# Sparse attention in a four-layer kernel: masked sums before head sums on VectorE, and a new order of the sums and gathers on GpSimd

## The reference, cut to what matters

```
iq = (x @ w_iq.T + b_iq).reshape(B, S, 4, 64);  ik = x @ w_ik.T + b_ik
iw = x @ w_iw.T + b_iw                                  # 4 weights for each query
head_scores  = relu(einsum('bqhd,bkd->bhqk', iq, ik))   # 4 heads, S x S each
index_scores = einsum('bhqk,bqh->bqk', head_scores, iw) # weighted sum of the heads
top_idx = top_k(index_scores, 32)
logits = einsum('bqd,bkd->bqk', rope(Q), rope(K)) * scale   # -inf where not in top_idx
x = x + softmax(logits) @ V @ w_o.T + b_o
```

## Time and profile before

| | us |
|---|---|
| median of 3 runs | 523.01 (522.72 to 523.64) |
| the profiled execution | 523.16 |
| its span, first to last instruction | 521.3 |

### The profile page before, as it was taken

The page is one execution under the profiler, slowest core; times in us unless marked ns, Lnnn a source line. Parts: engine busy times, 40 slices in busy tenths (PEclk is TensorE's granted clock), DMA queues, the critical chain, the costliest instruction groups (busy, mean ns, idle before and its releaser), DMA issues. The chain is left out here.

```text
span 521.3 us, 11629 instructions
## 1 busy us (share of the span) xinstructions
PE 437.5 (84%) x3048; PEld 383.1 (73%) x3048; DVE 377.2 (72%) x1501; ACT 337.8 (65%) x934; POOL 290.4 (56%) x329
## 2 busy tenths in 40 slices
PE   2689995799999896999988999998876599999981
PEld 1579894788988885667767777776655599988981
DVE  4789984836666651389999999999997656666661
ACT  1458882146766641899998999999782117666750
POOL 4763442067540005698878888887660027677752
PEclk9989996789999998999999999999996579999997
DMA  8942222124431111001111111111001213222210
GB/s 228 289 163 79 65 82 82 1 73 110 110 90 43 34 37 32 4 17 32 31 31 32 32 45 48 31 32 31 21 21 42 22 27 107 78 77 79 67 42 20
DMA packets 45070, 32.42 MB, mean 62 GB/s; under 512 B 13524, under 2 KB 39508, under 8 KB 45012
## 3 DMA queue, kind: packets, MB, share of 16 engines
q1 hardware_dynamic: 39892, 19.11, 13.1%
q0 software_dynamic: 5120, 12.62, 9.2%
HBM read 19.10 MB, written 12.62 MB: 61 GB/s over the span
## 5 line engine op out<-in xcount | busy, mean ns | idle before, releaser
L427 POOL DMA_INDIRECT big<-rows,gidx x64 | 61.6, 963 | 56.7 <-DVE gidx L1152 28.3
L639 PE MATMUL bank<-WE,hT 128*128 x624 | 83.6, 277 | 7.5 <-ACT hT L849 6.0
L629 PE MATMUL bank<-X,w 128*128 x624 | 83.4, 277 | 1.2 <-ACT X L836 0.4
L639 PEld LDWEIGHTS bank<-WE,hT 128*128 128x128 f32 x624 | 75.9, 192 | 9.6 <-issue 9.5
L629 PEld LDWEIGHTS bank<-X,w 128*128 128x128 f32 x624 | 75.8, 192 | 3.2 <-issue 3.1
L668 PE MATMUL bank<-xbT,WB 128*128 128x256 f32 x224 | 60.2, 400 | 9.3 <-ACT iq L890 8.7
L1184 DVE TENSOR_SCALAR hT<-bank,w 128x128 f32<-128x128 f32 x156 | 47.5, 346 | 22.7 <-PE bank L629 11.3
L841 ACT ACTIVATE w<-WE 128x644 f32 x78 | 57.2, 734 | 3.9 <-DVE big L1196 3.4
L447 POOL DMA_INDIRECT X<-x,pidx x32 | 31.7, 990 | 47.4 <-DMA x<-big 39.9
L836 ACT ACTIVATE X<-bank 128x128 f32<-128x128 f32 x64 | 17.8, 278 | 59.1 <-PE bank L620 58.9
L668 PEld LDWEIGHTS bank<-xbT,WB 128*128 128x128 f32 x224 | 40.1, 195 | 20.3 <-ACT iq L890 14.8
(11 more groups left out here) (164 smaller groups left out, 1025.0 us busy)
## 6 DMA issues: line engine op xcount, KB each, us to landing
WE<-w_experts SPq DMA_DIRECT2D x2, 2048.0 KB, 11.1
rows<-xf SPq DMA_DIRECT2D x32, 128.0 KB, 2.2
rows<-X SPq DMA_DIRECT2D x32, 128.0 KB, 2.6
X<-x SPq DMA_DIRECT2D x4, 512.0 KB, 7.7
x<-big SPq DMA_DIRECT2D x32, 64.0 KB, 1.5
big<-rows,gidx POOLq DMA_INDIRECT x64, 2.8
WB<-w_idx SPq DMA_DIRECT2D x1, 640.0 KB, 5.2
WE<-b SPq DMA_DIRECT2D x1, 512.0 KB, 12.2
```

What stands on the lines that cost most here:

```text
L427: pool.indirect_dma_start(xg[:, j, :], None, rows_dram[n], bass.IndirectOffsetOnAxis(ap=gidx[:, j:j + 1], axis=0)).then_inc(f["g"][j % G_R ...
L629: mm = pe.matmul(bank[r + 2 * (k // 2)][:, k % 2 * P:(k % 2 + 1) * P], w1[st.slot(1, 4)][:, k * P:(k + 1) * P], moving, start=True, stop=True)
L639: mm = pe.matmul(bank[4 + r][:, 0:D], hT[r][:, k, :], WE[:, bass.ds(expert[(s - 2) % TURN], 1), W2_AT + k * D:W2_AT + (k + 1) * D].rearran ...
```

## The change

- VectorE: both masked sums stand first in a step. After them come both third sums and both fourth sums. The third sum of half 0 is no longer made one step earlier.
- GpSimd: the head sum of half 0 stands ahead of the rotation sum. The bias sum stands behind the gathers.
- The bias of the index weights is added by VectorE (`index_weights`, in `beside(1)`) as it takes them out of the accumulator. TensorE's one-row matmul and ScalarE's copy are gone. The bias is loaded with one transfer to all partitions in place of two to one row, and two waits on the loads count 64 in place of 80.
- TensorE: the first two turns of the probabilities stand behind the fourth projection. ScalarE waits for `iw` ahead of its first weighted heads in place of ahead of the scores.

```diff
@@ gpsimd, loop of the sparse attention
+                    add_heads(b, r, 0)
                     pool.wait_ge(b_["rp"], 2 * (b + 1))
                     after(pool, b_["S"], C * (b - 1))
                     pool.tensor_tensor(qr[r][:, :, :], qk[r][:, 0:2, :], qk[r][:, 2:4, :], ALU.add).then_inc(b_["qr"], 1)
-                    add_heads(b, r, 0)
                     add_heads(b, r, 1)
                 inverse_std(s)
+                if b + 3 < B:
+                    gather_x(b + 3)
                 if b < B:
                     pool.wait_ge(b_["xb"], b + 1)
                     pool.tensor_tensor(X[:, b * C:(b + 1) * C, :], X[:, b * C:(b + 1) * C, :],
                                        bo_bc[:, :].unsqueeze(1).to_broadcast([P, C, D]), ALU.add).then_inc(b_["xo"], 1)
-                if b + 3 < B:
-                    gather_x(b + 3)
@@ tensor
-                    turn_probabilities(b, r, 0)
                 if st.on(0, B):
                     project(3)
                 if st.on(2, B):
+                    turn_probabilities(b, r, 0)
                     turn_probabilities(b, r, 1).then_inc(b_["PT"], 1)
...
-                    pe.matmul(bank[5][:, S:S + C * IDX_HEADS], ones[0:1, :], rowc[:, 0:C * IDX_HEADS], start=True, stop=False)
@@ scalar
-                    act.wait_ge(b_["pj"], 5 * (b + 1))
-                    after(act, b_["wk"], C * (b - 1))
-                    act.activation(iw[r][:, :, :],
-                                   bank[5][:, S:S + C * IDX_HEADS].rearrange("p (c h) -> p c h", c=C),
-                                   ACT.Copy).then_inc(b_["iwe"], 1)
...
@@ vector
+            def index_weights(b, r):
+
+                dve.wait_ge(b_["pj"], 5 * (b + 1))
+                dve.tensor_tensor(iw[r][:, :, :], bank[5][:, S:S + C * IDX_HEADS].rearrange("p (c h) -> p c h", c=C),
+                                  biw_bc[:, :].unsqueeze(1).to_broadcast([P, C, IDX_HEADS]), ALU.add).then_inc(b_["iwe"], 1)
...
                 if st.on(2, B):
                     p, q = st.item(2), st.slot(2, 2)
                     mask_logits(0)
+                    mask_logits(1)
                 if st.on(1, B):
+                    b, r = st.item(1), st.slot(1, 2)
+                    after(dve, b_["pen"], C * (b - 1))
+                    add_third(b, r, 0)
                     add_third(b, r, 1)
                     add_fourth(0)
-                if st.on(2, B):
-                    mask_logits(1)
-                if st.on(1, B):
                     add_fourth(1)
                 def beside(i):
+                    if i == 1 and st.on(0, B):
+                        index_weights(st.item(0), st.slot(0, 2))
...
-                    if i == 3 and st.on(0, B):
-                        after(dve, b_["pen"], C * (st.item(0) - 1))
-                        add_third(st.item(0), st.slot(0, 2), 0)
```

More of the change, by code:

```diff
@@ L149, in build @@
         bv_rep = sb("bv_rep", [P, P])
-        rowc = sb("rowc", [1, C * IDX_HEADS])
+        biw_bc = sb("biw_bc", [P, IDX_HEADS])
         br_bc = sb("br_bc", [P, E])
@@ L325, in _ @@
             sp.dma_start(WR[:, :], w_router).then_inc(ld_w, 16)
-            for c in range(C):
-                sp.dma_start(rowc[:, c * IDX_HEADS:(c + 1) * IDX_HEADS], b_iw).then_inc(ld_w, 16)
+            sp.dma_start(biw_bc[:, :], b_iw.rearrange("a e -> (a e)").partition_broadcast(P)).then_inc(ld_w, 16)
             sp.dma_start(br_bc[:, :], b_r.rearrange("a e -> (a e)").partition_broadcast(P)).then_inc(ld_w, 16)
@@ L406, in _ @@
                     b, r = st.item(1), st.slot(1, 2)
-                    pool.wait_ge(ld_w, 80)
+                    pool.wait_ge(ld_w, 64)
                     pool.wait_ge(a_pt, b + 1)
@@ L547, in _ @@
                 if st.base == 6:
-                    pe.wait_ge(ld_w, 80)
+                    pe.wait_ge(ld_w, 64)
                 if st.on(6, B):
@@ L712, in _ @@
                     after(pe, tails[1]["xfT"], b - 3)
-                    pe.matmul(bank[5][:, S:S + C * IDX_HEADS], ones[0:1, :], rowc[:, 0:C * IDX_HEADS], start=True, stop=False)
                     for c in range(C):
                         mm = pe.matmul(bank[5][:, S + c * IDX_HEADS:S + (c + 1) * IDX_HEADS], xbT[r][:, c * P:(c + 1) * P],
-                                       WB[:, 9 * D:9 * D + IDX_HEADS], start=False, stop=(c == C - 1))
+                                       WB[:, 9 * D:9 * D + IDX_HEADS], start=True, stop=True)
                     mm.then_inc(b_["pj"], 1)
@@ L918, in _ @@
                     normalise_b(st, -1)
-                if st.on(0, B):
-                    act.wait_ge(b_["pj"], 5 * (b + 1))
-                    after(act, b_["wk"], C * (b - 1))
-                    act.activation(iw[r][:, :, :],
-                                   bank[5][:, S:S + C * IDX_HEADS].rearrange("p (c h) -> p c h", c=C),
-                                   ACT.Copy).then_inc(b_["iwe"], 1)
                 for c in range(C):
@@ L928, in _ @@
                             after(act, b_["hs"], C * (b - 1))
-                            act.wait_ge(b_["iwe"], b + 1)
                         for i in range(2):
@@ L935, in _ @@
                         act.wait_ge(b_["rel"], 2 * (C * b + c + 1))
+                        act.wait_ge(b_["iwe"], b + 1)
                         for h in range(2):
@@ L1294, in mask_logits @@
                                              ALU.add, ALU.min, lmin[q][:, c:c + 1]).then_inc(b_["ttr"], 1)
-                if st.on(1, B):
-                    b, r = st.item(1), st.slot(1, 2)
                 if st.on(2, B):
```

## The result

| | before | after |
|---|---|---|
| median of 4 runs, us | 523.33 (522.72 to 527.34) | 546.4 (545.32 to 548.64) |
| span of the profiled execution | 521.3 | 544.2 |
| granted clock of TensorE, whole span | 0.938 | 0.903 |
| start of the first gather to start of the last attention result | 207.64 | 231.02 |

The changed kernel is slower: the ratio is 1.0445, with an interval of 1.0404 to 1.0486. The time lies outside the range and on the other side of the forecast. The last row shows where: the stage of the sparse attention is 23.4 us longer, and that is the whole difference.

What follows compares the result with a forecast made beforehand. A loop of waits between VectorE and GpSimd was taken to set the 11.41 us step. Forecast: 523.16 - 1.9 (11 middle steps) - 1.6 (first steps) + 1.1 (last steps) = 520.8, so 520.6 as median; range 514.5 to 532.5.

Steps and rivals of the forecast that it cites:

- the bias sum asks at +3.97 us: GpSimd behind the gathers: bias sum ready 0.02 us behind the second `xf`, 0.23 ahead of `nb`, in every step.
- The ring: Sparse attention: GpSimd's whole program and VectorE's end of a step wait on each other, setting the 11.41 us step.
- the wait of the earlier trace: GpSimd waits for VectorE's aggregate `mv` once in each step, 14.6 us in 11 times.
- The step without collisions: VectorE's step: 11.41 - 1.20 + 0.40 + 0.10 = 10.71 us, a gain of 0.70.
- rival 1: Bias sum comes behind `nb`, so a step is 10.71 us and the total 514.8; chance 0.22.
- 1.1 us lost: Last steps with sums, no gathers left: bias sum among VectorE's sums, later `xf` meeting cosine and sine, net +1.1 us.
- The first steps: Steps where no `xf` or `nb` is in the way: about 1.6 us gained.
- the bound of 0.35: Gathers beside VectorE's third and fourth sums: slowed by nothing to 0.35 us, for one or both.
- the second half of 0.51 later at +3.95: VectorE's `xf`: first at +3.69 us from the first mask, second half at +3.95, `nb` at +4.20.
- `nb` waits for it, and the next MAX comes at +4.80: VectorE's `nb` waits for the bias sum; next MAX at +4.80 instead of +4.27, 0.53 us lost, step 11.24.
- rival 2: Bias sum gets in ahead of the second `xf`: 1.58 us lost, step 12.29, total 532.2; chance 0.26.
- a sign that the prediction had named: VectorE waiting for ScalarE's penalties, or for `pj` ahead of `iw`, would show the prediction wrong altogether.

Runs made afterwards that it cites:

- e2: The changed kernel, with GpSimd's bias sum made to wait until VectorE is through with `nb` and `xf`; ratio to the kernel before 0.9752.
- e3: The kernel before, with only GpSimd's head sum of half 0 moved ahead of the rotation sum; ratio 0.9878.
- e7: The kernel before, with only the index bias added on VectorE and the loads and turns that go with it; ratio 0.9984.
- e11: The kernel before, with the head sum of half 0 first and the index bias on VectorE; ratio 0.9963.
- e10: The changed kernel with the bias sum waiting for `nb` and `xf`, but index bias by one-row matmul and ScalarE copy as before; ratio to the kernel before 0.9851.
- e8: The kernel before, with VectorE's new order and GpSimd's cosine made to wait for `nb` and `xf`; ratio 0.9895.
- e9: The changed kernel with VectorE's old order, and the bias sum made to wait for `nb` and `xf`; ratio to the kernel before 0.9899.
- e5: The kernel before, with only the bias sum moved behind the gathers; ratio 1.0398.
- e6: The changed kernel with VectorE's old order put back; ratio to the kernel before 1.0496.
- e1: The changed kernel with the bias sum put back ahead of the gathers; ratio to the kernel before 1.0444.
- e4: The kernel before, with only VectorE's new order of masks, third sums and fourth sums; ratio 1.0454.
- e12: The changed kernel with `nb` put ahead of `xf` on VectorE; ratio to the kernel before 1.0483.
- V: The part that gives VectorE its new order: both masks first, then both third and both fourth sums; alone on the kernel before, ratio 1.0454.
- B: The part that moves GpSimd's bias sum behind the gathers; alone on the kernel before, ratio 1.0398.
- I: The part that adds the index bias on VectorE, with all that goes with it; alone on the kernel before, ratio 0.9984.
- H: The part that puts GpSimd's head sum of half 0 ahead of the rotation sum; alone on the kernel before, ratio 0.9878.

## Why the prediction was wrong

The forecast said: the bias sum asks at +3.97 us, right behind the second `xf`, `nb` waits for it alone, the step is 11.24. I take its steps in turn, counted from the start of the first mask (303.40 in the slow step shown).

**Right: what the change takes away.** The ring is open: the wait of the earlier trace rows is gone. The step without collisions was worked out as 10.71, and e2, which takes out the collision alone, measures 10.67. Its stage is 12.75 us shorter than before, where rival 1 said 8.2. The rest came from the last four spacings (39.76 in place of 43.41), since its waits keep the meetings away there too, where I had counted 1.1 us lost. The first steps gained what was forecast: the first mask of the first step with all its parts came at 236.44 in place of 238.54, 2.1 us ahead, 1.6 said.

**Right: the lists up to `xf`.** The power left alone takes 1.03 (1.04 said), and the first `xf` comes at +3.69 (+3.69 said). The two gathers start at +1.68 and +3.16. The first takes 1.18 beside the two fourth sums in place of 1.04, within the bound of 0.35 that I gave. So the bias sum starts at +4.13 in place of +3.97, by the prediction's own count still between the second `xf` and `nb`.

**Failed first: "the second half of 0.51 later at +3.95".** The second `xf` starts at +4.25, behind the bias sum. In e2 it is at 304.75 - 300.81 = +3.94, as worked out. Something held VectorE during the second gather. The prediction put this at nothing without a reason: it took `xf` at its free length of the earlier trace rows beside any gather. Its sentence "`xf` and `nb` already run beside gathers and neither of those grows" asks only whether the gathers grow, and it was drawn from the wrong gather as well. In the earlier trace rows `xf` at 299.19 lies in the first gather, behind which stands another gather, and `nb` at 299.70 has begun before the second. Nowhere before does `xf` run in the second gather, behind which stands a sum. The runs divide by just this:

| `xf` in a gather | behind the gather stands | pair takes |
|---|---|---|
| before, e3, e7, e11, at +0.60 | a gather | 0.59 |
| e2, e10, at +0.53 | the bias sum, which has to wait | 0.59 |
| e8, at +0.53 | the cosine, which has to wait | 0.59 |
| e9, at +0.05 | the bias sum, which has to wait | 0.59 |
| e5, e6, at +0.05 | the bias sum, free to go | 1.10 |
| after, at +0.53 | the bias sum, free to go | 1.28 or 3.75 |
| e1, e4, at +0.14 | the cosine, free to go | 3.42, and once 0.59 |
| e1, e4, at +0.53 | the cosine, free to go | 3.28 or 4.34 |
| e4, at +0.53 | the cosine, 2.2 to 2.4 us late by ScalarE | 0.58 |

The first column counts from the gather's start to that of the first `xf`. So it is not the gather that holds `xf`. A sum behind it in GpSimd's list, if nothing is left for it to wait for, already shuts VectorE out while the gather runs. e2 against after and e9 against e6 differ in nothing but those waits. What starts within 0.15 us of the gather's start still gets through (the first `xf` of e5, 0.34 us at +0.06); what starts 0.25 us later does not (its second, 0.85). The one pair of 0.59 us in e1 is no exception. The copy that its cosine waits for ends at 264.62, when both `xf` have begun (264.31 and 264.56), and `nb` behind them is caught. One difference stays open. With the bias sum behind the gather, what is held during the gather gets out when the gather ends (after, e5, e6). With the cosine behind it, it stands on until the sine is over (e1, e4).

**Failed next: "`nb` waits for it, and the next MAX comes at +4.80".** That is a lock by one sum, 0.53 us. In rival 2 too I had the held instruction get out after one sum, with 1.28 us more for `nb` by the cosine. The runs show another rule: among the sums it gets out only at the end of one whose successor has not been free to go for some 0.2 us (out at 0.16, held at 0.23, under e12). Bias sum, cosine and sine follow each other at once, so one `xf` stands through all three, 3.19 us. e5 shows that the forecast's own case would have come out no better: there `nb` was caught by the bias sum, just as the forecast had it, and stood for 3.13 us in every second step. Even with its first step right, the forecast's 0.53 lost would have been about 3 in such a step. I had taken "one sum" from the earlier trace rows, where `xf` gets out between cosine and sine (1.54) and `nb` is caught again (1.24). That was the rarer case, which a step without gathers shows in after as well (at 402.22 and 403.26, 1.12 and 1.30 us): in both the cosine had itself waited for ScalarE and started 0.08 us after it was released. Why the time since the release decides stays open.

**Rival 2: right by its event, not by its condition or its size.** The bias sum gets in ahead of the second `xf` and the step is longer than before, as rival 2 said. But it was to come if the bias sum asked before +3.95. It started at +4.13, later than forecast, and the second `xf` was late by the hold, so that the right direction of rival 2 is in part luck. It was priced at 1.58 us a step, with a step of 12.29 and 532.2 in all. A slow pair of `xf` alone loses 3.16 (3.75 against 0.59). The eleven pairs of after lose 3.07 - 0.59 = 2.48 on average. With the 10.67 of e2 that makes 13.15 of the measured 13.54, so that nearly all of the loss is VectorE's. The 0.4 us that are left have room for what follows from it: VectorE waits 2.4 us in 5 times for ScalarE's penalties, a sign that the prediction had named, and the granted clock of TensorE is 0.88 in the middle of the stage in place of 1.00. No run separates these two.

The page "SBUF — State Buffer" of the Trainium skill, section "Who interferes with whom", which the prediction quoted against the change, was right in kind: the loss is this lock. What it says, a lock for the whole of one instruction, gives 0.72 us for the bias sum here; measured were 3.19, for three in a row.

**Two smaller slips.** The third sum of 0.48 us in the earlier trace rows (296.21) does not stand beside a tiny operation alone: it began first, and the power at 296.34 ran beside it. And the net of +1.1 us for the last steps does not follow from its terms: two steps of 1.8 less one of 2.0 are 1.6, and 0.9 with the 0.7 gained. Measured were 1.5 over the last four spacings.

**Chances.** By the rows that I had, 0.02 us lay between forecast and rival 2, and both were priced from one escape in the earlier trace rows. The range should have reached to a lock through all three sums: 0.72, 1.34 and 1.26 us by the earlier trace rows, 3.3 in a step.

## What to carry to other kernels

Where two engines shut each other out, look at the place of each instruction in the other's list, not only at what it waits for. If several of the one engine's instructions stand in a row with nothing to wait for, price a collision at the whole row, and count the instruction ahead of the row to it. A wait on the engine with slack that lets the other's short instructions through first is cheap (0.38 us here, all hidden) and can turn a loss into the gain that the reordering was worth.

## What the runs showed of the hardware that was not expected

- A VectorE instruction of the `xf` or `nb` kind stood through three GpSimd sums in a row: 3.19 us after, 3.13 in e5, for 0.33 and 0.15 when free. The size of the held instruction made no difference between these two.
- Whether VectorE got in between two such sums went by how long the cosine had been free to go when it started: at 0.16 us or less (e12) VectorE got in, at 0.23 us or more (after) it did not.
- A sum of GpSimd that is free to go holds VectorE already while the gather ahead of it runs: 1.10 us for two `xf` in e6, 0.59 in e9, where the sum has a wait in front.
- A gather that starts beside VectorE's fourth sums takes 1.08 to 1.18 us in after in place of 1.04.
- Parts of the change do not add: V 1.045 and B 1.040 alone, 1.045 with all; I is worth nothing alone and 0.27 us a step in e2, while H with I in e11 gains 0.0037 of the time where H alone gains 0.0122.
